# First attention and FFN run in one stage, the FFN five tiles behind

## The reference

```python
x = x + _L0_xattn_ref(norm(x), ctx, ctx, ...)   # 64x64 projections over the channel axis, 8 heads
x = x + _L0_ffn_ref(norm(x), ...)

# in _L0_xattn_ref
scores = jnp.einsum('hbdk,hbek->hbde', qh, kh) * scale
p = jax.nn.softmax(scores, axis=-1)
xh = jnp.einsum('hbde,hbek->hbdk', p, vh)
# in _L0_ffn_ref
xq = int4_quant(x)                        # factor: mean of |x| over the row
gate = bitlinear(xq, w_gate, s_gate); up = bitlinear(xq, w_up, s_up)
inter = int8_quant(up * jnp.square(jax.nn.relu(gate)))   # factor: max of |.| over the row
return bitlinear(inter, w_down, s_down)   # weights ternary, 512 -> 1376 -> 512
```

## Time and profile before

| | before |
|---|---|
| median of 3 runs | 761.53 us |
| the profiled execution | 762.43 us, its span 760.6 us |
| busy share of the span | PE 90%, DVE 82%, ACT 64%, POOL 52% |
| attention stage, about 223 to 320 us | PE busy 63.9 of the 96.8 us from 223.8 |
| FFN stage, about 320 to 443 us | PE busy 78.5 of the 78.9 us from 343.0 |
| granted TensorE clock | 0.975 over the span |

### The profile page before, as it was taken

The page is one execution under the profiler, slowest core; times in us unless marked ns, Lnnn a source line. Parts: engine busy times, 40 slices in busy tenths (PEclk is TensorE's granted clock), DMA queues, the critical chain, the costliest instruction groups (busy, mean ns, idle before and its releaser), DMA issues. The chain is left out here.

```text
span 760.6 us, 17982 instructions
## 1 busy us (share of the span) xinstructions
PE 680.8 (90%) x6734; PEld 354.0 (47%) x6761; DVE 623.7 (82%) x975; ACT 487.6 (64%) x902; POOL 397.6 (52%) x337
## 2 busy tenths in 40 slices
PE   5999999999977667599999869999999999958998
PEld 2454555555545555344444324444444444425643
DVE  6878788978736668689999768999999999959675
ACT  3888866666615666577767527878878788753320
POOL 2000009999944577332212328677677687739730
PEclk9999999999999999899999969999999999989999
DMA  6234545556334324023343300000000000024505
GB/s 169 77 115 155 202 164 166 133 148 170 86 93 119 61 71 81 9 52 61 78 78 58 68 11 1 1 2 1 1 2 1 1 2 1 1 43 90 92 33 189
DMA packets 94186, 54.93 MB, mean 72 GB/s; under 512 B 78549, under 2 KB 78549, under 8 KB 94101
## 3 DMA queue, kind: packets, MB, share of 16 engines
q1 hardware_dynamic: 93348, 53.25, 27.0%
q10 hardware_dynamic: 752, 0.52, 0.3%
HBM read 32.20 MB, written 4.19 MB: 48 GB/s over the span
## 5 line engine op out<-in xcount | busy, mean ns | idle before, releaser
L1427 POOL TENSOR_TENSOR query_qn<-query_eq,query_rq 128x1024 f32<-128x1024 f32 x64 | 122.0, 1906 | 53.4 <-DVE query_rq L1363 51.4
L681 ACT ACTIVATE keys_ek<-keys_psK,keys_mk 128x512 f32<-128x512 f32 x128 | 86.9, 684 | 39.2 <-DVE keys_mk L533 37.3
L533 DVE TENSOR_REDUCE keys_mk<-keys_psK 128x2 f32<-128x1024 f32 x64 | 77.9, 1217 | 16.8 <-PE keys_psK L740 16.6
L1354 DVE TENSOR_REDUCE query_mq<-query_psQ 128x16 bf16<-128x1024 f32 x64 | 75.5, 1180 | 5.1 <-PE query_psQ L1515 4.9
L1360 DVE TENSOR_REDUCE query_lq<-query_eq 128x16 f32<-128x1024 f32 x64 | 77.2, 1207 | 2.3 <-ACT query_eq L1446 2.2
L1446 ACT ACTIVATE query_eq<-query_psQ 128x1024 f32<-128x1024 f32 x64 | 65.2, 1019 | 21.2 <-PE query_psQ L1528 21.2
L1537 PE MATMUL query_psX<-all_ident,query_qn 128*128 128x128 f32 x512 | 70.8, 282 | 0.4 <-ACT query_qT L1453 0.4
L751 PE MATMUL keys_psT<-all_ident,keys_ek 128*128 128x128 f32 x512 | 70.8, 282 | 0.0
L763 PE MATMUL keys_psG<-keys_eT,keys_cT 128*64 128x512 f32 x256 | 69.0, 617 | 1.0 <-issue 0.9
L751 PEld LDWEIGHTS keys_psT<-all_ident,keys_ek 128*128 128x128 f32 x512 | 55.5, 142 | 28.2 <-issue 20.0
L1453 ACT ACTIVATE query_qT<-query_psX 128x1024 f32<-128x1024 f32 x64 | 65.4, 1023 | 1.1 <-PE query_psX L1537 1.1
(11 more groups left out here) (268 smaller groups left out, 1492.1 us busy)
## 6 DMA issues: line engine op xcount, KB each, us to landing
all_ring<-in_L_ffn_w_down_dram SPq DMA_DIRECT2D x8, 688.0 KB, 4.5
all_ring<-in_L_ffn_w_gate_dram SPq DMA_DIRECT2D x10, 512.0 KB, 4.7
all_ring<-in_L_ffn_w_up_dram SPq DMA_DIRECT2D x10, 512.0 KB, 3.8
all_x_res<-in_x_dram SPq DMA_DIRECT2D x4, 1024.0 KB, 5.6
att_ctx_n<-in_ctx_dram SPq DMA_DIRECT2D x16, 256.0 KB, 3.1
out_dram<-all_x_res SPq DMA_DIRECT2D x16, 256.0 KB, 2.1
all_cf<-in_ctx_dram SPq DMA_DIRECT2D x15, 256.0 KB, 2.7
att_w_nat<-in_L_ffn_W_dram SPq DMA_DIRECT2D x4, 256.0 KB, 4.3
```

The source lines that it names most:

```text
L533: dve.tensor_reduce(mk[:, c, :], psK[c % 2][:, :, :], X, ALU.max, negate=True).then_inc(mk_ok, 1)
L681: act.activation(ek[t % 2][b][:, c, :], psK[c % 2][:, b, :], ACT.Exp, bias=mk[:, c, b:b + 1], accum_out=le[t % 2][:, b, c:c + 1]).then_inc ...
L1354: dve.tensor_reduce(mq[g % 2][:, :, 0:HEADS], psQ[g % 2][:, :, :].rearrange("p b (h d) -> p b h d", d=D), X, ALU.max, negate=True).then_in ...
L1427: pool.tensor_tensor(qn[m % 2][:, :, :], eq[m % 3][:, :, :], rq[m % 2][:, :].unsqueeze(2).broadcast_to([P, 2 * HEADS, D]), ALU.mult).then_ ...
```

## The change

The two stages become one, `attention_and_ffn`, of 24 steps. In step i tile i is attended and tile j = i - 5 goes through the FFN; steps 0 to 4 only attend, 16 to 20 only feed, 21 to 23 finish the last downs. With that:

- The factors of the FFN input are worked out for two tiles at a time, eight times, instead of for 4 and for 12. What doesn't depend on the tile moves to `scale_constants`, once.
- The first operation of `quantise` goes from DVE to POOL (`scaled_x`); rounding works in place.
- PSUM: psQK stays a pair; from step 5 on scores, projection, output and values take turns on one pair (psA); four banks remain for the FFN, one gate, one down, two up. From FFN tile 12 on the gate blocks use psQK as well. `rounded` and Square work in place (h, r).
- The deviation and statistics of a tile come one step earlier. The late weights' work on POOL begins at step 5 (before: 2); the fourth block of W and Bmat are loaded later, into buffers used before; the three FFN scale factors are loaded in the key stage, in which the small bias rows are made two steps later.

```diff
-FORE_FF = 4
+LAG = 5
+GROUP = 2
+def scaled_x(pool, k, i):
+    f = k.ff
+    wait(pool, f.xq_ok, i)
+    pool.tensor_scalar(f.y[:, :], k.x[:, i, :], k.mv[:, i, 0:1], k.s4[:, i:i + 1], ALU.subtract, ALU.mult).then_inc(f.y_ok, 1)
...
@@ gpsimd @@
+            for i in range(STEPS):
+                j = i - LAG
+                if feeds(j - 1):
+                    rounded(j - 1)
+                if attends(i + 2):
+                    normed(i + 2)
+                if feeds(j + 1):
+                    scaled_x(pool, k, j + 1)
+                if attends(i):
+                    attention(i)
+                if finished(i):
...
+                    end_x(pool)
+                    pool.wait_ge(ab_ok, i - 1)
+                    sums_s(pool)
+                    products_s(pool)
                 if W_STEP <= i < ROW_STEP:
                     later_weights(pool, k, scaled_ok, whi_ok, wlo_ok, w_in, i - W_STEP)
...
@@ vector @@
+                if attends(i):
                     shifted(i)
+                if feeds(j - 3):
+                    fed(j - 3)
+                if attends(i):
+                    sums(i)
+                if feeds(j):
+                    gated(j, 0)
+                if feeds(j - 3):
+                    stats(j - 3, sixF, xf_ok, stf_ok, mvf_ok)
+                if attends(i - 1):
+                    attended(i - 1)
+                if feeds(j + 1):
+                    quantise(dve, k, j + 1)
+                if attends(i - 1):
+                    stats(i - 1, sixA, xa_ok, sta_ok, mva_ok)
+                if finished(i):
+                    sums_s, inverse_s, products_s = scales_of[i // GROUP - 1]
                     inverse_s(dve)
+                if feeds(j):
+                    gated(j, 1)
+                    gated(j, 2)
+                    scales(j)
...
@@ scalar @@
+                if feeds(j):
+                    gate(j, 0)
+                if attends(i):
                     exponentials(i)
+                if feeds(j):
+                    squared(j, 0)
+                    if attends(i - 1):
+                        projected(i - 1)
+                    if feeds(j - 1) and attends(i):
+                        rounded(j - 1)
+                if attends(i + 1):
                     heads(i + 1)
+                if feeds(j):
+                    gate(j, 1)
+                    squared(j, 1)
+                if attends(i + 1):
                     values(i + 1)
+                if feeds(j):
+                    gate(j, 2)
+                    squared(j, 2)
...
+                if attends(i - 1):
+                    deviation(i - 1)
...
@@ tensor @@
+                if attends(i):
                     scores(i)
+                if feeds(j):
+                    up(j, 0)
+                if attends(i - 1):
                     projected(i - 1)
+                if attends(i + 1):
                     projections(i + 1)
+                if attends(i - 1):
                     outputs(i - 1)
+                if feeds(j):
+                    up(j, 1)
+                if attends(i + 1):
                     values(i + 1)
+                if feeds(j):
+                    up(j, 2)
+                if feeds(j - 2):
+                    down(j - 2)
...
@@ sync @@
+                if feeds(j - 1):
+                    turn_h(j - 1)
...
+                if i >= W_STEP + 2 and (i - W_STEP) % 2 == 0 and (i - W_STEP - 2) // 2 < NC:
+                    turn((i - W_STEP - 2) // 2)
+                if feeds(j + 1):
+                    wait(sp, u_ps, NB * j)
+                    turn_x(sp, k, j + 1)
```

More of the change, by code:

```diff
@@ L52 @@
 READY = 3
+LATE_W = 3
 def chunk(ap, c, n=P):
@@ L155, in products @@
[L155 to L159, removed]
+        pool.tensor_scalar(k.sg[:, tiles], beta, k.ffw[:, 0:1], None, ALU.mult).then_inc(f.sc_ok, 1)
@@ L275, in later_loads @@
     loads = []
-    for c in range(NC):
-        loads.append((late.w_nat[:, c, :], a["W1"][c * P:(c + 1) * P, :]))
+    for c in range(LATE_W):
+        loads.append((late.w_nat[c][:, :], a["W1"][c * P:(c + 1) * P, :]))
     for q in range(4):
@@ L890, in attention0, with attends, feeds, started @@
         loads = later_loads(nc, a, k)
         late_each = 4
+        block = s.block()
+        def attends(i):
+            return 0 <= i < TILES
+        def feeds(j):
+            return 0 <= j < TILES
+        def started(i):
+            return i % GROUP == 0 and 0 <= i // GROUP - 1 < GROUPS
+        def finished(i):
+            return i % GROUP == 1 and 0 <= i // GROUP - 1 < GROUPS
+        def values_at(i):
+            return psF[:, 2:4, LOW] if i <= LAG else psA[:, :, LOW]
+        def projected_at(t):
+            return psF[:, 0:2, LOW] if t + 1 < LAG else psA[:, :, LOW]
@@ L1033, in deviation, with gate, squared @@
                                accum_out=k.xabs[:, t:t + 1]).then_inc(ab_ok, 1)
+            def gate(t, n):
+                w = FFB[n][1] - FFB[n][0]
+                q = NB * t + n
+                act.wait_ge(g_ps, q + 1)
+                wait(act, h_ok, q - 2)
+                act.activation(r[n][:, 0:w], gate_bank(t, n)[:, 0:w], ACT.Relu, scale=k.sg[:, t:t + 1]).then_inc(r1_ok, 1)
+            def squared(t, n):
+                w = FFB[n][1] - FFB[n][0]
+                act.wait_ge(r1_ok, NB * t + n + 1)
+                act.activation(r[n][:, 0:w], r[n][:, 0:w], ACT.Square).then_inc(r2_ok, 1)
@@ L1035, in _, with rounded @@
+            def rounded(t):
+                act.wait_ge(hr_ok, t + 1)
+                wait(act, hT_in[t % 2], 16 * (t // 2))
+                act.activation(hq[t % 2][:, 0:FF], h[t % 2], ACT.Identity, bias=k.m_minus[:, :]).then_inc(hq_ok, 1)
             heads(0)
             values(0)
-            for i in range(TILES + 2):
-                if 0 <= i - 1 < TILES:
+            act.wait_ge(pad_ok, 2)
+            for i in range(STEPS):
+                j = i - LAG
+                if finished(i):
+                    begin_x, act_x, end_x = factors[i // GROUP - 1]
+                    act_x(act)
+                if attends(i - 1) and not feeds(j):
@@ L1108, in _, with down @@
+            def down(t):
+                pe.wait_ge(hT_in[t % 2], 16 * (t // 2) + 16)
+                wait(pe, xf_ok, t)
+                for m in range(FFC):
+                    w = min(P, FF - m * P)
+                    mm = pe.matmul(psD, hT[t % 2][0:w, m, :], k.wdT[0:w, m, :], start=m == 0,
+                                   stop=m == FFC - 1)
+                mm.then_inc(d_ps, 1)
             projections(0)
             values(0)
-            for i in range(TILES + 1):
-                if i < TILES:
+            for i in range(STEPS):
+                j = i - LAG
+                if attends(i):
```

516 lines of the change are left out of this document (219 added, 297 removed).

## The result

The changed kernel takes 780.81 us (median of 4 runs, 779.68 to 783.19) where the kernel before, on the same chip, takes 761.54: a ratio of 1.0252, interval 1.0232 to 1.0271. It is slower by 19 us, and the forecast of 746, with its range of 739 to 758, is wrong on the side that had 0.11.

A forecast was written before the change was run, and what follows sets the result against it. Attention filled no engine (5.44 us a tile), the FFN filled PE (7.03). Merged, the parts sum to 302.0 + 11 T, 427.4 at T = 11.4 against 443.0, a gain of 15.6 us: about 746 us, range 739 to 758.

The forecast's parts named there:

- Steps 17 to 20: FFN-only steps of the merged loop: 7.03 us each as before, 28.1 in all, with PE's 7.0 the limit.
- the sentence about SyncE: SyncE's transposes in a mixed step: x issued in time unless all come together, then PE waits into its own slack.
- T, the period of a mixed step: Length of each step attending one tile and feeding another: 11.4 us, between 10.8 and 12.8.
- The ring of the prediction: Mixed step: DVE max and subtraction, ten ACT operations, DVE's third product, max of h to next free slot: 10.8 us.
- Step 5: First mixed step, with no rounding yet: T less 1.4, predicted 10.0 us.
- Step 16: Step with the last projection and output beside the FFN: 8.0 us.
- The end: From the last factor of the rounding to the last statistics, same chain as before, with the rest of that step: 10.5 us.
- No issue gaps at all: Rival: long matmuls let the instruction queue fill, T is 10.9, gain 21.1 us, time 740.4; chance 0.16 (below 742).
- Waits add up: Rival: port waits and issue gaps lengthen mixed steps, T 12.3, gain 5.7 us, time 755.8; chance 0.15 (751 to 760).
- PE is starved of instructions: Rival: instruction gaps on PE in mixed steps, T up to 15.0, slower by 24 us, 786; chance 0.11.
- The mixing does nothing: Rival: attention waits stay unshared, T 12.5, gain 3.5 us, time 758; counted within the 0.15 of "Waits add up".
- Port waits: DVE's two rounding instructions in mixed steps waiting for POOL: 0 to 0.9 us, charged nothing; by the skill T nearer 12.

The follow-up runs named there:

- e7: Changed kernel with SyncE issuing x ahead of h, GpSimd scaling x by addition and ahead of its rounding of h: 754.22 us, ratio 0.9915 to the kernel before.
- e2: Changed kernel with SyncE's order kept, ACT rounding h early in the steps without attention too: 763.75 us, ratio 1.0037 to the kernel before.
- e1: Changed kernel with only SyncE's order changed, next tile's x transposed ahead of h: 761.64 us, ratio 0.9995 to the kernel before.
- e8: e1 with the down product using 6 of its 11 chunks, less work for PE: 758.61 us, one run.
- e4: e1 with ACT rounding h at the end of every step: 758.11 us, ratio 0.9964 to the kernel before.
- e9: e8 with ACT rounding h at the end of every step as well: 760.59 us, one run.
- e13: e7 with the maximum of h over its first 512 columns and the down product using 6 of 11 chunks: 744.45 us, one run.
- e5: e1 with GpSimd scaling x by addition and ACT rounding h at the end of every step: 755.92 us, ratio 0.9940 to the kernel before.

## Why the prediction was wrong

**The step that failed: "Steps 17 to 20 are FFN alone, 7.03 each as before, 28.1".** They took 53.8. It rested on the amount of PE's work, which was right (e7: 29.1), and on the sentence about SyncE, that x is issued in time for the next step and PE would otherwise wait into its own slack. That sentence was argued for a mixed step, where ACT rounds early; it was never asked of the steps without attention, where the same queue stands but the rounding is last. The diff has both facts: `turn_h(j - 1)` ahead of `turn_x(j + 1)` on SyncE, and on ACT the early rounding only `if feeds(j - 1) and attends(i)`; the other case, at the end of the step, is the line that e2 changes. And in the loops x is taken one tile ahead in place of two, which the prediction didn't notice. e1 and e2 each take one half of the ring away, and each gives the 17 to 19 us back.

**The clock was not in the sum.** The prediction took each matmul at its length in a PE that is never idle. The waits for x let the granted clock fall to 0.81 in the window 388 to 451, and matmuls of 1.03 us took up to 1.91. So a wait cost PE more than its length. Steps 17 to 20 of e7 (394.35 to 423.45) show the split of PE's time: busy 27.5 of 29.1 us at a granted clock of 1.00, against 38.2 of 53.8 at 0.78 in the kernel after. Of the 24.7 us between them 10.6 are busy time, the same work at the lower clock, and 14.0 are idle time. What the ring would be at the full clock no run shows, since its length holds slow matmuls too.

**T, the period of a mixed step: right in size, for a wrong reason.** 11.4 was forecast and 11.38 found once x was in time (11.80 on average over steps 6 to 14 of the kernel after, with its x waits; step 15, which has no next tile to project, takes 10.26 and was priced at a full T). The ring of the prediction closed over ACT, at 10.8. In e8 the ten ACT operations reach from 321.89 to 329.05, 7.16 us in place of the 6.7 of the sum, and the difference is ACT waiting for PE's groups (its values start at 327.29, when PE's matmuls of 326.56 are done, its third Relu behind those of 327.16). That ACT's path isn't the limit e4 and e9 show, by taking 1.43 us out of it without effect. The limits were the ring through PE's groups (11.38) and PE itself (11.28 to 11.35). PE's 10.8 of work and the half of the old issue time that was added, 0.5, make 11.3, near what e7 shows of PE alone (11.03 busy and 0.32 of issue). That the forecast of T held is luck: the sum was of another ring, and the half-and-half guess added to it fell on PE's floor. The sign that was named for the ring, one large wait of DVE for ACT's last Square, is there in e7 (1.20 us), but it doesn't tell the two rings apart: one through PE's groups gives DVE the same wait.

**Step 5: "T less 1.4", predicted 10.0, was 14.9.** The 1.4 us that it takes off are those of the rounding, and e4 and e9 show that the rounding doesn't set a step. And the first x was priced at 0 to 2.6 us, in steps 0 to 4; PE stood for it in step 5, and longer:

```profile
259.00 1.49 PE L1322 MATMUL mid_psF<-all_wgT,all_ff_xT 128*128 128x512 bf16 x3 [4.55 <-DMA all_ff_xT<-all_ff_xq]
260.28 1.64 PE L1327 MATMUL mid_psF<-all_wuT,all_ff_xT 128*128 128x512 bf16 x4
```

4.55 us for the first x, and the slow matmuls behind it (1.64 for what takes 1.03). Steps 0 to 4 themselves took 27.4 against 27.2. No version here repaired step 5; it takes 13.4 to 15.9 in all of them, and it is most of what is left between e7 and the forecast.

**The other terms.** Step 16: 8.0 was forecast without a working, and 9.2 to 9.3 is measured in nearly every version. The end: 10.5, measured 11.3.

**The rivals.** *No issue gaps at all* (T 10.9): falls, with 11.38 measured; in e7 PE still stands 2.7 us in issue between 283 and 378, 0.3 a step. *Waits add up* (T 12.3): the kernel after has 11.80 on average, but by its waits for x (5.3 us between 283 and 378), and 11.38 without them. *PE is starved of instructions*: it falls as the cause. Dense runs of 64x64 matmuls still show a gap now and then, 0.89 us in one of nine steps in e13, in a step of 11.70 in place of 10.48, and nothing like it in every step. The slow result came by a mechanism that the prediction named only in its last line ("if the transposed x lands late in most steps") and gave no price or chance. *The mixing does nothing*: falls; a tile of attention and one of FFN take 11.38 us together where they took 5.44 + 7.03 = 12.5 apart. *Port waits*: they are there. DVE's rounding took 1.27 us beside GpSimd in e8 where it takes 0.43 alone, and they didn't reach T: the step is 11.38 in e7 too, where the same instruction takes 0.43. The rows of this step (timeline of e8, DVE and POOL):

```profile
325.54 0.64 DVE L188 TENSOR_SCALAR all_ff_y<-all_ff_y 128x512 f32<-128x512 f32 x1
325.84 1.35 POOL L347 TENSOR_TENSOR mid_w_lo<-mid_w_nat,mid_w_hi 128x512 f16<-128x512 f32 x1
326.21 1.27 DVE L191 TENSOR_SCALAR all_ff_xq<-all_ff_y 128x512 bf16<-128x512 f32 x1
```

By the rule of the Trainium skill (SBUF — State Buffer, Who interferes with whom) T was to come near 12. The 1.27 agrees with a lock that is waited for, the 11.38 shows that here the wait was not on the path.

Against the sum "302.0 + 11 T" the version e7 ends 7.9 us later, 205.7 in place of 197.8: 5.5 in step 5, 1.3 in step 16, 1.0 in the FFN-only steps, 0.9 in the end, 0.3 in the mixed ones, and 1.0 back in steps 0 to 4. That is what the idea was worth with x in time: 754.2 in place of the 746 of the forecast, and 6 us under the kernel before.

**What stays open.** In e1, e2, e5, e7 and e8 step 7 takes 12.9 to 13.0 us in place of 11.38; in e7 the short step 15 gives most of it back, so the ten steps still add up to the forecast. Step 6 has no down product yet, so PE comes into step 7 early, by the 2.5 us of that product, and stands. In e5 and e7 it stands 2.41 us for the subtraction, and the matmuls behind it are slow (e7):

```profile
283.77 0.69 PE L1298 MATMUL mid_psA<-all_wT,mid_pn 64*64 64x64 f32 x32 [2.41 <-DVE mid_sh L1078]
...
285.52 1.10 PE L1260 MATMUL mid_psQK<-all_wT,mid_ctx_n 64*64 64x64 f32 x32
286.37 1.10 PE L1309 MATMUL mid_psA<-mid_v,mid_wp 64*64 64x64 f32 x32
```

The granted clock from 282.21 to 288.90 is 0.74, and 1.00 before and behind. In e1, e2 and e8 it stands 2.4 to 2.8 us for x instead, with the same slow matmuls behind. Where it stood 1.51 us (e13), or 1.10 and later 1.47 (the kernel after), they were at full length and the step wasn't long. That is read from the rows; no run was made for it.

## What to carry to other kernels

When stages are merged, walk every queue once for each kind of step: the full ones, and the steps that fill and drain the merged loop. A queue of DMA issues is a ring member like any engine: a transfer that is needed soon must not stand behind one whose source is made last in the step, and a distance of two tiles that becomes one has to be priced as a term. When two limits lie within 0.1 us of each other, an experiment that shortens one of them shows nothing, and only both together show either.

## What the runs showed of the hardware

- GpSimd's `tensor_scalar` on 128x512 f32 took 2.09 us with subtract and multiply, and 0.77 us with add and multiply, the operands otherwise alike: the same tile and two per-row scalars, one of which comes from another tile. Which of the two (the operation or the scalar's place) makes the difference wasn't separated.
- A wait on TensorE costs more than its length when the clock falls in it: behind a wait of over 4 us four matmuls of 128x512 took 1.89 in place of 1.03, and a window with such waits was granted 0.81, between the levels of 1.2 and 2.4 GHz; the same steps without them 1.00.
- TensorE's groups have a price of order: before the first and the second gate of a mixed step, bf16 groups behind a group of 64x64 f32 matmuls, stand 0.16 us of "issue" (319.22 and 324.96 in e8), and none before the third. With 11.03 us of busy time (e7) they make up its floor in a mixed step (11.28 to 11.35).
